# Gated MLP with product-key experts: the low weight parts cut in three pieces on GpSimd, the choice of experts in two halves on VectorE

## What is computed

```python
def _L1_ffn_ref(hidden_states, W_q, keys, down_embed, up_embed, gate_w, up_w, down_w):
    x = hidden_states.reshape(n, h)                      # n = 2048 tokens, h = 512
    queries = (hidden_states @ W_q).reshape(2, n, RETRIEVAL // 2)
    routing = jnp.einsum('tnd,tdk->tnk', queries, keys)  # 2 x 64 keys
    scores2, idx2 = jax.lax.top_k(routing, TOP_K)        # TOP_K = 8
    all_scores = (sx[:, :, None] + sy[:, None, :]).reshape(n, TOP_K * TOP_K)
    all_idx = (ix[:, :, None] * NUM_KEYS + iy[:, None, :]).reshape(n, TOP_K * TOP_K)
    scores, pk = jax.lax.top_k(all_scores, TOP_K)
    indices = jnp.take_along_axis(all_idx, pk, axis=-1)
    de = down_embed[indices]
    ue = up_embed[indices]
    ew = jnp.einsum('nh,nkh->nk', x, de)
    ew = jax.nn.silu(ew) * jax.nn.softmax(scores, axis=-1)
    experts_states = jnp.einsum('nk,nkh->nh', ew, ue).reshape(b, s, h)
    mlp = jax.nn.silu(x @ gate_w) * (x @ up_w) @ down_w  # inner width 2048
    return mlp.reshape(b, s, h) + experts_states
x = x + _L1_ffn_ref(_layernorm(x, axis=-1), ...)
```

## Time and profile before

| | us |
|---|---|
| median of 3 runs | 2130.06 (2127.67 to 2131.92) |
| the profiled execution, its own time | 2134.1 |
| its span, from first to last instruction | 2132.3 |
| TensorE (PE) busy | 2021.3 (95%) |
| VectorE (DVE) busy | 1301.5 (61%) |
| ScalarE (ACT) busy | 795.0 (37%) |
| GpSimd (POOL) busy | 564.8 (26%) |
| mean granted TensorE clock | 0.975 of full speed |

### The profile page before, as it was taken

How to read it: one execution, slowest core, us unless ns; L and a number is a source line. 1 busy time by engine, 2 the same in 40 slices (tenths; PEclk the granted TensorE clock), 3 DMA queues, 4 the chain that set the end, 5 groups by cost and what they waited for, 6 DMA issues and landing times. The chain is left out here.

```text
span 2132.3 us, 33595 instructions
## 1 busy us (share of the span) xinstructions
PE 2021.3 (95%) x12656; PEld 1658.1 (78%) x12656; DVE 1301.5 (61%) x2249; ACT 795.0 (37%) x2370; POOL 564.8 (26%) x552
## 2 busy tenths in 40 slices
PE   6999999999999989999989999998388999999998
PEld 5888888888888878888877777775277888778777
DVE  5555555655555554424344677775557788876787
ACT  5555555755555532111123454453123221222121
POOL 3222221321233226101022233232102323332331
PEclk9999999999999989999999999999699999999999
DMA  6000000200021012101041000000311455545545
GB/s 242 29 7 5 5 5 17 75 30 27 30 70 57 23 60 89 50 10 59 15 144 62 12 22 22 15 23 16 120 40 53 139 197 178 179 147 176 175 146 196
DMA packets 78566, 158.31 MB, mean 74 GB/s; under 512 B 8849, under 2 KB 31121, under 8 KB 78481
## 3 DMA queue, kind: packets, MB, share of 16 engines
q0 software_dynamic: 23712, 87.04, 12.2%
q1 hardware_dynamic: 54768, 70.17, 10.0%
HBM read 140.41 MB, written 16.78 MB: 74 GB/s over the span
## 5 line engine op out<-in xcount | busy, mean ns | idle before, releaser
L48 PE MATMUL four_banks<-xT_all,m_w_hi 128*128 (+1 forms) x1024 | 321.4, 395 | 1.1 <-PEq L1898 1.1
L48 PEld LDWEIGHTS four_banks<-xT_all,m_w_hi 128*128 128x128 f32 x1024 | 192.5, 188 | 46.8 <-issue 1.2
L2244 POOL DMA_INDIRECT ring<-in_table,x_row x128 | 123.6, 966 | 328.8 <-DVE y_all L2344 281.8
L48 PE MATMUL four_banks<-xT_all,m_w_lo 128*128 (+1 forms) x512 | 202.3, 395 | 0.0
L1118 DVE TENSOR_SCALAR f_relu<-bank,f_b 128x512 f32<-128x512 f32 x64 | 47.9, 749 | 168.8 <-ACT f_h_hi L1061 168.8
L511 ACT ACTIVATE prob<-four_banks,mx,rms 128x128 f32<-128x128 f32 x256 | 114.0, 463 | 92.1 <-DVE mx L645 92.1
L1061 ACT ACTIVATE f_h_hi<-bank,f_b 128x512 fp32r<-128x512 f32 x64 | 44.1, 689 | 259.4 <-PE bank L48 259.4
L2334 DVE SCALAR_TENSOR_TENSOR x_junk<-x_in,y_ln,ring 128x512 bf16<-128x512 f32 x128 | 126.2, 1020 | 11.9 <-DMA ring<-in_table,x_row 10.6
L289 POOL TENSOR_TENSOR rms<-ssq,constants 128x8 f32<-128x8 f32 x64 | 13.0, 204 | 436.2 <-ACT junk L496 263.4
L2221 ACT ACTIVATE x_act_of<-x_dot,y_ln 128x2 f32<-128x2 f32 x64 | 18.9, 296 | 260.4 <-DVE x_junk L2334 258.3
L1781 DVE TENSOR_REDUCE l_roped<-four_banks 128x16 f32<-128x2048 f32 x32 | 73.4, 2293 | 69.5 <-PE four_banks L1468 69.5
(11 more groups left out here) (290 smaller groups left out, 5349.3 us busy)
## 6 DMA issues: line engine op xcount, KB each, us to landing
f_stage<-in_w POOLq DMA_DIRECT2D x14, 512.0 KB, 4.4
f_x_in<-x SPq DMA_DIRECT2D x18, 256.0 KB, 2.9
ctx_in<-in_ctxT SPq DMA_DIRECT2D x32, 128.0 KB, 2.5
x_in<-in_x SPq DMA_DIRECT2D x16, 256.0 KB, 2.6
x<-xres SPq DMA_DIRECT2D x16, 256.0 KB, 2.0
x<-l_res SPq DMA_DIRECT2D x16, 256.0 KB, 2.1
m_stage<-in_gate SPq DMA_DIRECT2D x8, 512.0 KB, 10.5
m_stage<-in_up SPq DMA_DIRECT2D x8, 512.0 KB, 10.0
```

The lines of the kernel that those rows point to most:

```text
L48: mm = pe.matmul(out, st, mv, start=first and n == 0, stop=last and n == len(terms) - 1)
L2244: pool.indirect_dma_start(ring[:, slot, :], None, table, bass.IndirectOffsetOnAxis(ap=row[:, tile_of(g), k:k + 1], axis=0)).then_inc(S[f"g ...
```

## The change

In each pair, ScalarE's `cut` comes one half-step earlier, after h = 8p + 2. GpSimd's `cut_lo` is three instructions of 128 x 1024 (gate, up, down weights in turn), one each behind the fetches under h = 8p + 3, 8p + 4 and 8p + 5; each adds 1 to `w_cut`, and all who wait for it count in threes (CUTS). `choose` ends where the softmax's differences are ready, which now come ahead of the table rows; the rest is `find_rows`, after the second `multiply` of the step.

```diff
-    ROUTES = 4
+    ROUTES, CUTS = 4, 3
...
                 if pair >= 2:
-                    sp.wait_ge(S["w_cut"], pair - 1)
+                    sp.wait_ge(S["w_cut"], CUTS * (pair - 1))
...
-            pe.wait_ge(S["w_cut"], 1)
+            pe.wait_ge(S["w_cut"], CUTS)
             step(NC, 0, 1, 0)
...
                     pair = 2 * o + slot
-                    pe.wait_ge(S["w_cut"], pair)
+                    pe.wait_ge(S["w_cut"], pair * CUTS)
                     step(pair * NC, 0, slot, 1 - slot)
...
                     for g in taken[2 * n + j]:
                         silus(g)
-                if n % NC == 1 and n // NC + 1 < PAIRS:
-                    cut(n // NC + 1)
+                    if j == 0 and n % NC == 1 and n // NC + 1 < PAIRS:
+                        cut(n // NC + 1)
...
-            def cut_lo(pair):
+            def cut_lo(pair, i):
                 pool.wait_ge(S["w_hi"], pair)
-                pool.tensor_tensor(wp[pair % 2][1][:], stage[:], wp[pair % 2][0][:], ALU.subtract).then_inc(S["w_cut"], 1)
+                third = slice(i * NG, (i + 1) * NG)
+                pool.tensor_tensor(wp[pair % 2][1][:, third], stage[:, third], wp[pair % 2][0][:, third], ALU.subtract
+                                   ).then_inc(S["w_cut"], 1)
...
-                if n % (2 * NC) == 3 and n // (2 * NC) + 1 < PAIRS:
-                    cut_lo(n // (2 * NC) + 1)
+                if n % (2 * NC) in (3, 4, 5) and n // (2 * NC) + 1 < PAIRS:
+                    cut_lo(n // (2 * NC) + 1, n % (2 * NC) - 3)
...
                 then(dve.tensor_copy(halff[:], half[:]))
+                dve.tensor_tensor(best[:], best[:], total[:, 0, :].unsqueeze(2).to_broadcast([P, 4, TOP]), ALU.subtract
+                                  ).then_inc(S["below"], 1)
+
+            def find_rows(g):
+
+                tiles = slice(4 * g, 4 * g + 4)
                 for i in range(2):
...
-                    if i == 0:
-                        dve.tensor_tensor(best[:], best[:], total[:, 0, :].unsqueeze(2).to_broadcast([P, 4, TOP]), ALU.subtract
-                                          ).then_inc(S["below"], 1)
...
-                    if j == 0 and n < ROUTES:
-                        choose(n)
+                    if n < ROUTES:
+                        (choose, find_rows)[j](n)
```

## The result

| | before | after |
|---|---|---|
| median of 4 runs, us | 2130.64 (2127.67 to 2131.92) | 2173.02 (2168.85 to 2178.7) |
| ratio | | 1.0204, 95% interval 1.019 to 1.0219 |
| profiled execution, its own time | 2134.1 | 2171.68 |
| its span | 2132.3 | 2169.9 |
| start of the last stage in the span | 1573.6 | 1571.4 |

Two executions that took far longer than the rest (4096.92 us, one of four in experiment 9, and 2330.99 us, of the kernel before beside it) are left out of what follows.

A forecast was written before the change was run, and what follows sets the result against it. TensorE was taken to bound the last stage, idling 12.6 us for VectorE. Terms -10.0 + 28.5 + 12.3 + 0.5 = +31.3 us on the median 2130.06 gave 2161 us, range 2143 to 2171.

The forecast's parts named there:

- later gaps of before removed: TensorE's five later gaps from VectorE stalls beside the cut go, with restarts and slow clock: -10.0 us.
- first four steps, to E(9): First pair, until TensorE starts h = 8's down products: split choice makes VectorE's step 18.1 us, before 15.8; +0.5 us.
- load waits: ScalarE's earlier high parts wait for weights in h = 10 and 42; TensorE idles 4.0 and 3.9 us; +12.3 in all.
- ends of pairs, idle: TensorE waits for GpSimd's late third piece at the ends of pairs 1 to 6: 19.3 us.
- ends of pairs, restart and slow clock: After those six waits, restarts cost 1.8 us and slow clock 7.4 us, none behind the two 2 us waits.
- What the pieces add: Part on TensorE's waits for the third piece at pairs' ends: +28.5 us with restarts and slow clock.
- M(8p+6) + 7.6 + 3.0: Third piece's earliest start: VectorE's half-step 8p + 6 begins at M, additions end 7.6 us later, piece 3.0 after that.
- Pair 1: At this pair's end TensorE waits 2.1 us for the third piece, VectorE being on time.
- Pair 4: Two groups in h = 36; pieces delay prod_lo of 37 by 0.8 and dots of 38 by 0.7; wait 2.7 us.
- Pair 5: VectorE is 2.4 us late at h = 46 after the load wait and held 0.8 there; wait 5.0 us.
- the second load wait: In h = 42 the load is issued in the same half-step and takes 8.8 us; TensorE idles 3.9 us.
- My likeliest case: Both load waits and late third pieces at pairs' ends bite: 2161 us, own range 2152 to 2170, chance 80%.

The follow-up runs named there:

- experiment 9: Changed kernel with pieces one and two both under 8p + 3 and the third left under 8p + 5; 2179.21 us, ratio 1.0249.
- experiment 4: Kernel before with only the three pieces under 8p + 3, 4, 5, high parts and choice as before; 2156.29 us, ratio 1.0126.
- the first four experiments: Changed kernel with late high parts (2160.84 us) or with a later wait for the third piece (2135.78); kernel before with split choice (2132.13) or pieces (2156.29) alone.
- experiment 6: Kernel before with the subtraction as three instructions back to back under 8p + 3; 2126.94 us, ratio 0.9988.
- experiment 1: Changed kernel with ScalarE's high parts back after h = 8p + 3, pieces and split choice kept; 2160.84 us, ratio 1.0136.
- experiment 3: Kernel before with the split choice of experts alone; 2132.13 us, ratio 1.0012.

## Why the prediction was right in its way and too low in its size

Forecast 2161 (2143 to 2171), measured 2173.02, 2 us outside the range; the forecast change was +31 us, the measured one +42. Every kind of mark that I had named came, though some lay outside the bounds: six gaps by GpSimd (2.36 to 6.75 us, where I had named 2 to 5), two load waits with ScalarE idle (gaps of 5.11 and 2.26 us for "near 4"), no x_junk over 3.26 us (3.1 named), and VectorE waiting 2.21 us for Silu in three of the four first steps, 4.87 in the second. The sum, term by term, in the profiled executions:

| term | forecast | measured |
|---|---|---|
| later gaps of before removed | -10.0 | -10.0 |
| first four steps, to E(9) | +0.5 | +0.8 |
| load waits | +12.3 | +10.8 |
| ends of pairs, idle | +19.3 | +27.0 |
| ends of pairs, restart and slow clock | +9.2 | +11.6 |
| sum | +31.3 | +40.2 |

The stage as a whole grew by 39.8 us. **The step that failed is the sum of TensorE's waits at the pairs' ends, in "What the pieces add": 19.3 us forecast, 27.0 measured. Its largest error is the placing of the second piece**, which I took as free in pair 1: M(8p+6) + 7.6 + 3.0 for the third piece holds only if the second does not touch half-step 8p + 6 ahead of its additions. That makes 3.2 of the 7.7 us. By pair, forecast and measured: 2.1 and 5.31, 2.0 and 2.36, 4.9 and 5.49, 2.7 and 4.22, 5.0 and 6.75, 2.6 and 2.84.

- *Pair 1, +3.2.* VectorE and GpSimd around half-steps 13 and 14 of the changed kernel:

```profile
1705.35 1.54 DVE L2349 SCALAR_TENSOR_TENSOR y_all<-ring,x_coef,y_all 128x512 f32<-128x512 f32 x2
1707.99 0.69 DVE L2276 TENSOR_TENSOR m_gated<-m_gated,four_banks 128x512 f32<-128x512 f32 x1 [1.10 <-PE four_banks L48]
1709.38 3.50 DVE L2278 TENSOR_TENSOR m_prod_lo<-m_gated,m_prod_hi 128x512 fp32r<-128x512 f32 x1 [0.70 <-ACT m_prod_hi L2212]
...
1709.90 2.41 POOL L2250 TENSOR_TENSOR m_w_lo<-m_stage,m_w_hi 128x1024 fp32r<-128x1024 f32 x1
...
1721.40 2.35 POOL L2250 TENSOR_TENSOR m_w_lo<-m_stage,m_w_hi 128x1024 fp32r<-128x1024 f32 x1
```

VectorE had ended its group at 1706.89, and then stood 1.1 us until TensorE gave it half-step 14. The piece runs 3.0 us after that end, whether VectorE has gone on or not, so it met prod_lo, which took 3.50 instead of 0.69: 2.8 us. I had tied the piece to M(14). With the pieces alone (experiment 4) the same two came the other way round, prod_lo first, and the gap of pair 1 was 2.81 us, not 5.31:

```profile
1697.42 0.69 DVE L2278 TENSOR_TENSOR m_prod_lo<-m_gated,m_prod_hi 128x512 fp32r<-128x512 f32 x1 [0.70 <-ACT m_prod_hi L2212]
...
1698.20 2.41 POOL L2250 TENSOR_TENSOR m_w_lo<-m_stage,m_w_hi 128x1024 fp32r<-128x1024 f32 x1
...
1709.44 0.79 PE L48 MATMUL four_banks<-xT_all,m_w_hi 128*128 128x512 f32 x1 [2.81 <-POOL m_w_lo L2250]
```

A quarter of a microsecond decides it: the piece began 0.52 us behind the start of prod_lo in the changed kernel, and 0.78 us behind it, with prod_lo done, in experiment 4. Experiment 9 is the test by an edit, with the price of its own that is told there.

- *Pair 4, +1.5.* Half-step 37 held two delays for one: its prod_lo took 1.60, and then an x_junk stood 1.03 us for a row of the table:

```profile
1919.96 1.16 POOL L2244 DMA_INDIRECT ring<-in_table,x_row  x1 [0.30 <-issue]
1921.14 2.42 POOL L2250 TENSOR_TENSOR m_w_lo<-m_stage,m_w_hi 128x1024 fp32r<-128x1024 f32 x1
...
1925.82 0.75 DVE L2339 SCALAR_TENSOR_TENSOR x_junk<-x_in,y_ln,ring 128x512 bf16<-128x512 f32 x1 [1.03 <-DMA ring<-in_table,x_row]
```

  The fetches issued around here took 4.2 to 5.8 us to land. So the row that x_junk stood for is that of the fetch at 1919.96, ahead of the piece, and not of the next one at 1923.72, behind it, which could not have landed in 2.1 us. By the program too the dots of this group wait for the fetch that the group three before it released, and with two groups in h = 36 VectorE was at these dots 6.1 us after that release. I had no term for VectorE waiting for its rows. Before, the cut had held VectorE in this half-step for longer than the row needed.
- *Pair 5, +1.8, and the second load wait, -1.6.* The two belong together. The load took 7.0 us in h = 42 (1972.64 to 1979.63), not 8.8, and TensorE idled 2.26 and 0.45 us instead of 3.9, with no slow clock. From M(42) to M(46) were 40.5 us (1966.30 to 2006.84), where my sum has 41.9, so VectorE came 1.4 us sooner; TensorE had lost 2.8 us less by then. By this reckoning, made from one trace, the other 1.4 us moved to the pair's end. The first load took 8.8 us, where I had 7.9, and its gap was 5.1 for 4.0.
- *Everywhere, +0.2 to 0.35.* A piece takes 2.35 to 2.43 us, not a third of 6.84, and TensorE starts 0.15 after it. Of the 0.6 us of pair 3 this leaves some 0.3 without a cause found.

ScalarE's rows for the two loads, with the SP queue's issues:

```profile
1674.16 0.46 SPq L2127 DMA_DIRECT2D m_stage<-in_gate  x1
...
1682.98 2.77 ACT L2204 ACTIVATE m_w_hi<-m_stage 128x3072 fp32r<-128x3072 f32 x1 [8.89 <-DMA m_stage<-in_down]
...
1972.64 0.44 SPq L2127 DMA_DIRECT2D m_stage<-in_gate  x1
...
1979.63 2.78 ACT L2204 ACTIVATE m_w_hi<-m_stage 128x3072 fp32r<-128x3072 f32 x1 [7.06 <-DMA m_stage<-in_down]
```

**The clock** was the second term too small. I let the gaps of 2 us go free, by the row of 1.68 us. The gap of 2.36 us cost 7.39 - 5.61 = 1.8 us; the granted clock behind it was 0.57 on average, between the levels of 1.2 and 2.4 GHz:

```profile
1795.00:1799.00 4.00, 4.00 (x12) 3.14 (x11) 3.08 (x8) 0.30 (x1) 1.83 (x2) 0.57 0.58 176
```

The price hardly went by the length of the gap: 1.7 to 1.9 us behind 2.36, 2.84, 4.22, 5.31 and 6.75 us, and 2.7 behind 5.49. My likeliest case's own range held such losses of clock; the lateness of the second piece it did not hold. Its listed bounds also add up to some 2155 to 2172 us, and not to the 2152 to 2170 that I wrote.

**From the profile to the median.** I took 4.0 us off, because the profiled execution of before lay that much above its median. The one of after lies 1.3 below its own. The stage's start, ahead of which nothing was changed, lies between 1568.9 and 1574.3 us in the profiled executions of before, after and the first four experiments. Between before and after it differs by 2.2 us. So part of the 5.3 us between the two offsets lies ahead of the stage and has nothing to do with the change, and some 3 of the 12 us by which I was low are no error of the stage's sum (+40 measured, +31 forecast).

**The page and the row.** The Trainium skill ("SBUF — State Buffer", section "Who interferes with whom") has the first to issue hold the ports for its whole instruction. In the changed kernel too the prod_lo that began at 1709.38 stood still for the piece of 1709.90, whose length was the usual 2.41: by the start times of the profile the trace doesn't agree, as in the earlier trace rows. By that rule, which ends with each instruction, VectorE should come in between two pieces. In experiment 6 it did so in one of seven cuts (1.14 us for 5.55), and in the other six it stood for all three pieces. The runs don't show what decides between the two.

## What to carry to other kernels

Ask when an engine's program position is reached, not what number it bears: a queue paced by another engine's releases may lag by two steps, and work moved two places down it can pass the moment at which its reader asks. Splitting a long blocking instruction was right, but only with the pieces spread out: back to back they held VectorE as long as the whole in six of seven cuts. And a consumer that needs one third later than the others should wait for it later, too: for the kernel before with the pieces alone, either that wait or one place up the queue turned a loss of 1.3% into a gain of 0.7%. (In the changed kernel, with its early high parts and split choice, the later wait alone left a loss of 0.3%.) And don't move a reader of a load into the step that issues the load.

## What the runs showed of the hardware that I had not expected

- Two gaps of nearly the same length had different prices: 2.36 us, 1.8 us of lost time behind it; 2.26 us at 1985.11, none (the clock was 1.00 from 1985 to 1994 us). Before, 1.68 us had cost none and 2.89 us 1.4; in experiment 6 a gap of 1.94 us was followed by a granted clock of 0.66 (1897 to 1902 us). The runs don't show what decides between.

```profile
1985.00:1994.00 9.00, 8.60 (x36) 6.68 (x36) 7.92 (x18) 1.71 (x4) 3.77 (x4) 1.00 0.28 95
```

- The same three loads of 512 KB were there after 7.0, 8.8 and 11.4 us within the changed kernel (the last for pair 3, issued at 1743.59, where ScalarE stood 0.72 us for them). For the load of h = 10 alone it was 7.9 us before, 10.0 in experiment 1 and 10.7 in experiment 3. A forecast of such a wait needs a range of some us.
- VectorE's operation stood through three GpSimd instructions back to back in six of seven cuts, and came in after the first in one (experiment 6).
